# Two attention layers on one core: slots of two key chunks by 512 queries in place of one key chunk by 1024

## What is computed

```python
q = Wq @ x + bq            # 16 x 1024
k = Wk @ x + bk            # 16 x 1024
v = Wv @ x + bv            # 128 x 1024
energy = q.T @ k           # 1024 queries x 1024 keys
attn = softmax(energy, axis=keys)
x_next = gamma * (v @ attn.T) + x
```

## Time and profile before

| | us |
|---|---|
| time, median of 3 runs | 220.22 |
| lowest and highest of them | 219.42, 221.62 |
| span of the profiled execution | 219.6 |
| TensorE matmul busy in it | 203.2 (93%) |
| ScalarE busy | 167.8 (76%) |
| GpSimd busy | 160.0 (73%) |
| VectorE busy | 151.4 (69%) |

### The profile page before, as it was taken

One profiled execution on the slowest core, in us unless ns is written; L12 is line 12 of the kernel. 1 busy time (PEld: TensorE's weight loads), 2 busy tenths in 40 slices (PEclk: granted clock), 3 DMA queues, 4 the chain that ended last, 5 costly groups with the idle time before them and its releaser, 6 DMA issues.

```text
span 219.6 us, 2538 instructions
## 1 busy us (share of the span) xinstructions
PE 203.2 (93%) x874; PEld 116.7 (53%) x876; DVE 151.4 (69%) x145; ACT 167.8 (76%) x244; POOL 160.0 (73%) x87
## 2 busy tenths in 40 slices
PE   6766978797999999999999999999999999999994
PEld 1542423245565656565666466646564656565581
DVE  1599599674767777686768676867686749406972
ACT  2221479888999996999699969998799898958500
POOL 1780000069999799979997999799999957982950
PEclk9796799999999999999999999999999999999999
DMA  6807030009309200930075006600480710050202
GB/s 153 337 1 183 8 96 0 6 0 207 84 13 231 48 3 0 207 83 3 0 178 109 7 0 147 141 4 1 113 173 0 172 27 0 0 194 1 100 0 96
DMA packets 6142, 17.15 MB, mean 78 GB/s; under 512 B 1008, under 2 KB 1392, under 8 KB 6128
## 3 DMA queue, kind: packets, MB, share of 16 engines
q1 hardware_dynamic: 6128, 16.98, 30.9%
HBM read 2.69 MB, written 2.10 MB: 22 GB/s over the span
## 4 chain that ended last, share of the span: by engine, by line
PE 80%; DVE 11%; DMA 3%; issue 2%; ACT 2%; SPq 1%; ACTq 0%
PE out_psum L656 47%; PE ring L628 9%; PE ring L605 8%; PE ring L594 6%; PE ring L577 5%; DVE neg_max L494 5%; DMA x_all<-x_in 2%; PE out_psum L666 2%; DVE masked_hi L449 1%; ACT attn L399 1%; DVE shift_masked L502 1%; PE ring L618 1%; DMA q_shifted<-shift_rows 1%; DVE shift_rows L506 1%; DVE qk L454 1%
## 5 line engine op out<-in xcount | busy, mean ns | idle before, releaser
L348 POOL TENSOR_TENSOR attn_lo<-attn,attn_hi 128x1024 fp32r<-128x1024 f32 x45 | 110.2, 2467 | 10.0 <-ACT attn_hi L405 8.1
L494 DVE TENSOR_REDUCE neg_max<-ring 128x1 f32<-128x1024 f32 x64 | 76.2, 1220 | 27.3 <-PE ring L607 27.1
L379 ACT ACTIVATE ring<-ring,neg_max 128x1024 f32<-128x1024 f32 x64 | 69.8, 1090 | 19.1 <-DVE neg_max L494 18.8
L399 ACT ACTIVATE attn<-ring 128x1024 f32<-128x1024 f32 x64 | 62.9, 1022 | 11.1 <-PE ring L630 11.1
L342 POOL TENSOR_SCALAR attn_hi<-attn 128x1024 fp32r<-128x1024 f32 x22 | 24.1, 1094 | 30.2 <-ACT attn L399 30.2
L605 PE MATMUL ring<-qk_swapped,qk 64*128 64x512 f32 x64 | 28.7, 466 | 6.6 <-DVE qk_swapped L454 4.2
L656 PE MATMUL out_psum<-attn_hi,v_hi 128*128 128x512 f32 x96 | 33.8, 433 | 0.0
L656 PE MATMUL out_psum<-attn,v 128*128 128x512 f32 x64 | 31.4, 614 | 0.0
L656 PE MATMUL out_psum<-attn_hi,v_lo 128*128 128x512 f32 x96 | 30.0, 394 | 0.0
L656 PE MATMUL out_psum<-attn_lo,v_hi 128*128 128x512 f32 x96 | 29.9, 393 | 0.0
L607 PE MATMUL ring<-qk,qk_swapped 64*128 64x512 f32 x64 | 28.7, 466 | 0.0
(11 more groups left out here) (50 smaller groups left out, 214.1 us busy)
## 6 DMA issues: line engine op xcount, KB each, us to landing
q_shifted<-qk SPq DMA_DIRECT2D x16, 256.0 KB, 4.5
k_twice<-qk SPq DMA_DIRECT2D x16, 256.0 KB, 5.2
qk_swapped<-qk SPq DMA_DIRECT2D x14, 256.0 KB, 3.4
out_dram<-x_all SPq DMA_DIRECT2D x8, 256.0 KB, 2.5
x_all<-x_in SPq DMA_DIRECT2D x3, 512.0 KB, 7.3
x_all<-x_in SPq DMA_DIRECT2D x2, 256.0 KB, 4.8
late<-late_in SPq DMA_DIRECT2D x1, 384.0 KB, 6.5
q_shifted<-shift_rows SPq DMA_DIRECT2D x16, 8.0 KB
```

Of the source, the lines that this page charges most:

```text
L348: nc.gpsimd.tensor_tensor(attn_lo[:, j - NATIVE], attn[:, j], attn_hi[:, j - NATIVE].bitcast(fp32), ALU.subtract).then_inc(lo_made["gpsimd ...
L379: nc.scalar.activation(e[:], e[:], ACT.Exp, bias=neg_max[s % 2][:, i:i + 1], accum_out=row_sum[s % 2][:, i:i + 1]).then_inc(sum_made, 1)
L399: nc.scalar.activation(attn[:, j], ring_tile("ET", s, k)[:], ACT.Exp).then_inc(attn_made, 1)
L494: nc.vector.tensor_reduce(neg_max[s % 2][:, i:i + 1], ring_tile("E", s, i)[:], axis=AX.X, op=ALU.max, negate=True).then_inc(max_made, 1)
```

## The change

A slot is now a pair of key chunks by 512 queries: slots 0 to 3 are the pairs 0, 1, 2, 3 for the first 512 queries, slots 4 to 7 the pairs 1, 2, 3, 0 for the other 512. Pair 0 is native, so slots 0 and 7 are native as before. A tile keeps its size (128 x 2 x 512), and a slot keeps its two or six matmuls of 512 columns; now the two matmuls of a pass have different weights (two key chunks) and all matmuls of slots 0 to 3 go to one bank of `out_psum`, those of slots 4 to 7 to the other. `finish(s,0)` waits for four slots, `finish(s,1)` for eight. TensorE waits for `finish(s-1,0)` before slot 0 and for `finish(s-1,1)` before slot 4. Two tables change: in `PE_STEP` `PV(0,3)` goes ahead of `QK(3)`, and in `DVE_STEP` `finish(0,0)` goes up, ahead of `mask(3)`.

```diff
-ORDER = [0, 2, 3, 4, 5, 6, 7, 1]
+PAIRS = [0, 1, 2, 3, 1, 2, 3, 0]
+SLOTS = TILES // 2
+def half_of(k):
+    return slice(k // SLOTS * HALF, (k // SLOTS + 1) * HALF)
+def native(k):
+    return PAIRS[k] == 0
...
 PE_STEP = [
-    ("QK", 3, 0), ("PV", 0, 3), ("ET", 1, 0), ("ET", 1, 1), ("PV", 0, 4), ("ET", 1, 2), ("ET", 1, 3),
+    ("PV", 0, 3), ("QK", 3, 0), ("ET", 1, 0), ("ET", 1, 1), ("PV", 0, 4), ("ET", 1, 2), ("ET", 1, 3),
...
 DVE_STEP = [
-    ("max", 2, 2), ("max", 2, 3), ("mask", 3, 0), ("cut", 1, 1), ("stack", 3, 0), ("max", 2, 4),
-    ("v_lo", 1, 0), ("max", 2, 5), ("max", 2, 6), ("max", 2, 7), ("finish", 0, 0), ("finish", 0, 1),
+    ("max", 2, 2), ("max", 2, 3), ("finish", 0, 0), ("mask", 3, 0), ("cut", 1, 1), ("stack", 3, 0), ("max", 2, 4),
+    ("v_lo", 1, 0), ("max", 2, 5), ("max", 2, 6), ("max", 2, 7), ("finish", 0, 1),
...
-        attn = sb("attn", [P, TILES, N])
+        attn = sb("attn", [P, TILES, 2, HALF])
...
             def finish(s, h):
-                dve.wait_ge(pv_half_mm if h == 0 else pv_mm, s + 1 if h == 0 else TILES * (s + 1))
+                dve.wait_ge(pv_mm, TILES * s + SLOTS * (h + 1))
...
             def energies_transposed(s, k):
-                nc.tensor.matmul(to[:, 0:HALF], k_twice[p][0:64, rows], q_shifted[p][0:64, 0:HALF],
-                nc.tensor.matmul(to[:, HALF:N], k_twice[p][64:128, rows],
-                                 q_shifted[p][64:128, HALF:N], start=True, stop=True).then_inc(et_mm, 1)
+                nc.tensor.matmul(to[:, 0:HALF], k_twice[p][0:64, first], q_shifted[p][0:64, part],
+                nc.tensor.matmul(to[:, HALF:N], k_twice[p][64:128, second],
+                                 q_shifted[p][64:128, part], start=True, stop=True).then_inc(et_mm, 1)
...
             def times_v(s, k):
-                p, j = s % 2, ORDER[k]
+                p, to = s % 2, out_psum[:, half_of(k)]
                 if k == 0:
                     pe.wait_ge(v_made, s + 1)
+                if k % SLOTS == 0:
+                    at_least(pe, x_made, 2 * (s - 1) + k // SLOTS + 1)
...
-                work = [(n, h) for n in range(len(passes)) for h in range(2)]
-                if k == TILES - 1:
-                    work.sort(key=lambda nh: nh[1])
-                for n, h in work:
-                    part = slice(h * HALF, (h + 1) * HALF)
-                    if k == 0 and n == 0:
-                        at_least(pe, x_made, 2 * (s - 1) + h + 1)
-                    if n == 2 and h == 0:
-                        wait_for_lo(pe, s, k)
-                    v, a = passes[n]
-                    last = nc.tensor.matmul(out_psum[:, part], v, a[:, part], start=(k == 0 and n == 0),
-                                            stop=(k == TILES - 1 and n == len(passes) - 1))
+                    passes = [(v[p][:, c + n], attn_hi[:, k - 1, n]) for v in (v_hi, v_lo) for n in range(2)]
+                    passes += [(v_hi[p][:, c + n], attn_lo[:, k - 1, n]) for n in range(2)]
+                for n, (v, a) in enumerate(passes):
+                    if n == 4:
+                        wait_for_lo(pe, s, k)
+                    last = nc.tensor.matmul(to, v, a, start=(k % SLOTS == 0 and n == 0),
+                                            stop=(k % SLOTS == SLOTS - 1 and n == len(passes) - 1))
                 last.then_inc(pv_mm, 1)
```

More of the change, by code:

```diff
@@ L200, in hi_on @@
         def hi_on(s, k):
-            if ORDER[k] < NATIVE:
+            if native(k):
                 return None
@@ L370, in add_bias0 @@
                         act.wait_ge(qk0_mm, 2 * n + h + 1)
-                        nc.scalar.activation(attn[:, n, part], ring_tile(use, 0, 0)[:, part], ACT.Identity,
+                        nc.scalar.activation(attn[:, n, h], ring_tile(use, 0, 0)[:, part], ACT.Identity,
                                              bias=weights[:, QK_SETS * P + bias:QK_SETS * P + bias + 1]
@@ L391, in attention @@
             def attention(s, k):
-                j = ORDER[k]
                 act.wait_ge(et_mm, TILES * s + k + 1)
-                if j < NATIVE:
+                if native(k):
                     at_least(act, pv_mm, TILES * (s - 1) + k + 1)
@@ L448, in _ @@
                         dve.wait_ge(stacked0_made, h + 1)
-                    nc.vector.tensor_scalar(masked_hi[:, part], attn[:, n, part], columns[:, mask:mask + 1], 0.0,
+                    nc.vector.tensor_scalar(masked_hi[:, part], attn[:, n, h], columns[:, mask:mask + 1], 0.0,
                                             ALU.mult, ALU.add).then_inc(masked0_made, 1)
@@ L453, in _ @@
                     dve.wait_ge(masked0_made, 2 * n + h + 1)
-                    nc.vector.tensor_tensor(to[:, part], attn[:, n, part], masked_hi[:, part].bitcast(fp32),
+                    nc.vector.tensor_tensor(to[:, part], attn[:, n, h], masked_hi[:, part].bitcast(fp32),
                                             ALU.subtract).then_inc(stacked0_made, 1)
@@ L622, in energies_transposed @@
             def energies_transposed(s, k):
-                p, j, to = s % 2, ORDER[k], ring_tile("ET", s, k)
-                rows = slice(j * P, (j + 1) * P)
+                p, to, part = s % 2, ring_tile("ET", s, k), half_of(k)
+                first, second = (slice((2 * PAIRS[k] + n) * P, (2 * PAIRS[k] + n + 1) * P) for n in range(2))
                 if k == 0:
@@ L633, in times_v @@
             def times_v(s, k):
-                p, j = s % 2, ORDER[k]
+                p, to = s % 2, out_psum[:, half_of(k)]
                 if k == 0:
                     pe.wait_ge(v_made, s + 1)
-                if j < NATIVE:
+                if k % SLOTS == 0:
+                    at_least(pe, x_made, 2 * (s - 1) + k // SLOTS + 1)
+                if native(k):
                     pe.wait_ge(attn_made, TILES * s + k + 1)
-                    passes = ((v32[p][:, j], attn[:, j]),)
+                    passes = [(v32[p][:, n], attn[:, k, n]) for n in range(2)]
```

34 lines of the change are left out of this document (13 added, 21 removed).

## The result

The change makes the kernel slower: 225.64 us (median of 4 runs, 224.84 to 226.32) against 220.37 us (4 runs, 219.42 to 221.62) for the kernel before; ratio 1.0235 [1.0198, 1.0273]. That is 5.3 us more where 2.95 were forecast. The profiled execution of the changed kernel took 224.84 us, with a span of 223.0. Lines are numbered anew: `mask` L471, `stack` L479, `v_lo` L497 (L489 before), `max` L502, `finish` L532, V L600 (L594 before), ET L634 and L636, GpSimd's `attn_hi` L352 and `attn_lo` L357.

What follows compares the result with a forecast made beforehand. It took TensorE's own sequence to bound the repeated steps. Stalls of 3.05 us less 0.1 us at the tail gave 2.95 us more, so 223.2 us from the median of 220.22; range 219.6 to 224.8 us.

Steps and rivals of the forecast that it cites:

- The moved QK: TensorE, five steps: `stack` ends later, so ET(s+1,2) waits for QK's ring tile, about 0.61 us each, 3.05 us.
- What stays: All engines: matmuls, weight loads, tile sizes, 64/128-row switches and DMAs stay, save earlier half 0 stores; cost nothing.
- what shortens another engine's chain gives nothing: Repeated steps: TensorE, busy 22.62 of 22.70 us, alone sets the pace; shorter chains elsewhere gain 0.
- the gain of 0 for GpSimd's earlier cut of x: Between stages 0 to 3: the cut starts 0.7 us earlier, but x already lay ready 5.0 us before QK.
- `finish(s,0)` ahead of `mask`: VectorE: finish runs after PV(s,3) and ends before `mask` is due; hidden, 0.7 us to spare.
- The boundary: Between stages: only one finish is left at the end, yet TensorE didn't wait there; gain 0, bound 2.8 us.
- The tail: End of the kernel: first finish and store go earlier, last store is alone; gain 0 to 0.5, taken as 0.1 us.
- The boundary pays: Rival, chance 0.19: GpSimd sets the pace, its earlier x cut gives 2.8 us in four stages; 220.4 us.
- Matmuls faster in one bank: Rival, chance 0.06: without alternating banks 288 cut matmuls give back up to 6.3 us; 216.9 us.
- Clock: Rival, chance 0.03: each TensorE stall brings a half-clock stretch costing 1.75 us, five times; 232 us.
- VectorE's queue: Rival, chance 0.06: late PV(s,3) makes finish hold `mask`, up to 0.7 us more per stall; 226.7 us.
- the ring: TensorE's wait at ET(s+1,2) for `stack` to free QK's ring tile: 3.05 us over five steps, chance 0.66.

Runs made afterwards that it cites:

- the last two kernels: GpSimd's second-layer cut of x also waits for `v32`: added to the kernel with `finish` in the gap, 221.04 us, 1.0022; added to the changed kernel, 223.76 us, 1.0132.
- `finish` in the gap: Changed kernel with QK ahead of PV(0,3) again and `finish(0,0)` between `max(2,5)` and `max(2,6)`: 223.45 us, 1.0158.
- QK first: Changed kernel with QK ahead of PV(0,3) again on TensorE, `finish(0,0)` left ahead of `mask`: 226.50 us, 1.0299.
- the swap alone: Kernel before with only `PV(0,3)` put ahead of `QK(3)` on TensorE: 225.33 us, 1.0241.

## Why the prediction was wrong

- **The moved QK: right.** Forecast 5 x 0.61 = 3.05 us, in the trace 2.9. Three kernels keep this stall and take away what the slow `v_lo` costs, in all steps or in four of five, each in its own way (`v_lo` earlier, `v_lo` short, GpSimd late): they lie 1.0149, 1.0154 and 1.0132 times above the kernel before, which is 3.3, 3.4 and 2.9 us.
- **The step that failed** is the one under "What stays": tiles "keep their sizes", "I cost all of this at nothing". I took an operation's duration as a property of its tile. `v_lo`'s depends on which engine starts first, and the change moved both: VectorE 0.62 later by the very stall that I had worked out, GpSimd 0.31 earlier. Sizes: 1.6 us more for `v_lo`, of which 0.3 to 0.44 per step reach TensorE in the changed kernel, 1.7 us in all. The upper end of my range had room for 0.3 more per step, but for no cause that I named.
- **The same mistake in another form** is "what shortens another engine's chain gives nothing", and the gain of 0 for GpSimd's earlier cut of x. It was right that it gains nothing. I never asked whether it could cost something; the last two kernels show that being early did.
- The Trainium skill has this rule ("SBUF — State Buffer", Who interferes with whom): a VectorE instruction with two inputs in SBUF contends with a GpSimd instruction that reads SBUF, and who issues first keeps the shared port for its whole length. The trace agrees: 3.05 us in the kernel with `finish` in the gap is the rest of GpSimd's 2.39 (2.24) and 0.8 behind it. It speaks against this change, and I hadn't weighed it.
- **`finish(s,0)` ahead of `mask`: right** in the changed kernel (84.50 to 85.25, `mask` at 85.88). It is hidden only as long as PV precedes QK: with QK first it holds `mask` and doubles the stall.
- **The boundary: right.** What shows it is not the kernel with the slots alone, which has both halves of `finish` at the end, but those with an early half and QK first: their steps with a fast `v_lo` keep 22.7 us and are no shorter, and with GpSimd held back the whole measures 1.0022. **The tail:** 0.06 us where I took 0.1.
- **Rivals.** The boundary pays: no. Matmuls faster in one bank: no, the slots alone measure 1.0017, and pairs stay 0.47 apart (210.18 to 210.65 in the changed kernel). Clock: not at an idle of 0.5 us; at 2.1 us it fell in two steps of five, for 1.5 us each time, near the 1.75 I had given it. VectorE's queue: `finish` held nothing, so this rival is wrong, though VectorE was late elsewhere. That the time I gave it, 226.7, is nearer to the result than my forecast is luck.
- **The numbers.** 225.64 - 223.2 = 2.4 us were missing. `v_lo` gives 1.7, of which the ring takes back 0.1. Of the 0.8 left, 0.15 is the median of before (220.37 for 220.22); the rest isn't in the traces and stays open. The profiled execution of the changed kernel is its fastest run (224.84), and 4.6 us of difference lie within the measured interval (4.4 to 6.0). The two spans differ by 3.4 us only, because the profiled execution of before came to step 0 1.15 us later (60.21 against 59.06), ahead of the steps that the change reorders. This did no harm to the forecast, since the sum stands on the median, but I read the span too lightly: 1.8 us lie around a span (224.84 - 223.0; 220.24 - 218.4 for the slots alone), so the span of 219.6 belonged to a run of about 221.4, not to the median.

It stays open how the 0.31 us by which GpSimd comes earlier divides between the early `finish` and the cut that no longer has to wait for `v_lo`: the swap alone, with `finish` untouched, has both orders in turn.

None of these kernels beats the one before.

## What to carry to other kernels

Before moving an instruction by some tenths of a microsecond, list the VectorE instructions that read two tiles in SBUF and start close to a GpSimd instruction that reads SBUF, and ask whether the move turns their order; a duration from the trace holds only for the order in which it was taken. A ring wait can be worked out from three rows (the due time of the writer, the end of the last reader, the handover); here it came out within 0.05 us. Then carry the stall on through the other engines' queues instead of stopping at its size. Where the same instructions show more busy time on an engine after a change, look there first.

## What the runs showed of the hardware

- In the kernel before `v_lo` takes 0.95 to 1.24 us where it starts ahead of GpSimd's cut. Where the cut starts 0.12 to 0.52 us ahead of it, here and in the changed kernels, it takes 2.7 to 3.1. In these, and where the cut was 1.5 us ahead (`v_lo` 1.74, QK first), `v_lo` ended 0.8 us behind the cut. The loser waits until the other's instruction ends, even for a sixth of the work (1.74 us for 128 columns).
- When VectorE wins, GpSimd's cut takes 2.97 in place of 2.39, and `attn_hi`, which reads one tile only, 1.76 in place of 1.05 (the kernel of before with `v_lo` earlier).
- So a program can fall into an alternation of fast and slow steps (22.7 and 23.9 us) with nothing in its tables that alternates.
- A TensorE idle of 0.5 or 1.2 us per step left the granted clock at 1.00; one of 2.1 us was followed by a lower grant (mean 0.70 over 3.6 us) in two of five steps, for 1.5 us each.
